# Five warm-up matmuls, not eight; GpSimd takes half of the first split; four maxima units and the projections of batch 1 change places

## What is computed

```python
def _L0_cond_ref(Efou, y, weight):
    ys = y * scale
    d = jax.lax.rsqrt(jnp.einsum('bi,io->bo', ys * ys, weight * weight) + EPS)
    return jnp.einsum('bsi,io->bso', Efou * ys[:, None, :], weight) * d[:, None, :]

def _L0_attn_ref(x, w_qkv, w_out):
    qkv = x @ w_qkv.T
    q, k, v = jnp.split(qkv, 3, axis=-1)
    ...
    q = _apply_rope(q.astype(jnp.float32), cos, sin).astype(x.dtype)
    k = _apply_rope(k.astype(jnp.float32), cos, sin).astype(x.dtype)
    scores = jnp.einsum('bhsd,bhtd->bhst', q, k) / scale
    scores = jnp.where(causal[None, None], scores, -jnp.inf)
    attn = jax.nn.softmax(scores.astype(jnp.float32), axis=-1).astype(x.dtype)
    out = jnp.einsum('bhst,bhtd->bhsd', attn, v)
    ...
    return out @ w_out.T
...
    x = x + _L0_attn_ref(_L0_cond_ref(x, cond_1024, L0_cond_weight), L0_attn_w_qkv, L0_attn_w_out)
    x = x + _L0_ffn_ref(_L0_cond2_ref(x, cond_1024, ...), ...)
```

## Time and profile before

| | |
|---|---|
| runs | 181.8, 184.19 and 183.96 us, median 183.96 us |
| span of the profiled execution | 180.1 us, from the first instruction to the last |
| what lies around the span | 1.7 us (to the fastest run) to 4.1 us (to the slowest); 3.9 us to the median |
| busy in the span | PE 169.0 us (94%), DVE 139.3 (77%), ACT 134.4 (75%), POOL 93.4 (52%) |
| chain that ended last | PE 70%, DVE 14%, ACT 8% of the span |

### The profile page before, as it was taken

The page is one execution under the profiler, slowest core; times in us unless marked ns, Lnnn a source line. Parts: engine busy times, 40 slices in busy tenths (PEclk is TensorE's granted clock), DMA queues, the critical chain, the costliest instruction groups (busy, mean ns, idle before and its releaser), DMA issues.

```text
span 180.1 us, 3258 instructions
## 1 busy us (share of the span) xinstructions
PE 169.0 (94%) x934; PEld 116.8 (65%) x934; DVE 139.3 (77%) x444; ACT 134.4 (75%) x224; POOL 93.4 (52%) x116
## 2 busy tenths in 40 slices
PE   6998989999999999988999999996999989999992
PEld 2765555765666666654648767874677867788881
DVE  5598899789898989981586998699889648637551
ACT  3569366687787788889735696953969999999970
POOL 4508188975453969696541632021769931676000
PEclk9999999999999999999999999999999999999999
DMA  4824673776666756421110799970760000001001
GB/s 132 305 46 103 179 208 118 231 257 233 177 203 187 198 181 184 157 78 49 58 55 9 217 294 361 338 229 11 234 233 0 0 4 0 0 2 58 0 4 58
DMA packets 15349, 24.28 MB, mean 135 GB/s; under 512 B 2844, under 2 KB 4828, under 8 KB 15308
## 3 DMA queue, kind: packets, MB, share of 16 engines
q1 hardware_dynamic: 14532, 23.29, 42.0%
q10 hardware_dynamic: 800, 0.79, 1.7%
HBM read 18.71 MB, written 5.27 MB: 133 GB/s over the span
## 4 chain that ended last, share of the span: by engine, by line
PE 70%; DVE 14%; ACT 8%; issue 5%; POOL 1%; ACTq 0%; DVEq 0%; POOLq 0%
PE psum L1405 11%; PE psum L1538 10%; PE psum L1466 9%; PE psum L1539 9%; PE psum L1540 9%; PE psum L1441 7%; DVE psum L772 4%; PE psum L1341 2%; PE psum L1355 2%; PE psum L1287 2%; ACT t_probs L1105 2%; PE psum L1445 2%; DVE t_raw L924 1%; PE psum L1400 1%; ACT t_q_pad L1155 1%
## 5 line engine op out<-in xcount | busy, mean ns | idle before, releaser
L772 DVE CUSTOM_DVE_ANT_0 psum<-psum,t_causal 128x128 f32<-128x128 f32 (+3 forms) x128 | 58.8, 525 | 6.0 <-PE psum L1405 3.3
L1105 ACT ACTIVATE t_probs<-psum 128x1024 f32<-128x1024 f32 (+2 forms) x48 | 40.8, 883 | 8.4 <-PE psum L1441 5.5
L1405 PE MATMUL psum<-t_stacked,t_q_pad 96*128 96x256 f32 (+2 forms) x104 | 32.1, 378 | 2.4 <-DVE t_row_max L772 1.2
L1405 PEld LDWEIGHTS psum<-t_stacked,t_q_pad 96*128 96x128 f32 x104 | 17.7, 188 | 16.3 <-DVE t_row_max L772 11.2
L672 POOL TENSOR_SCALAR_AFFINE_SELECT t_probs<-t_probs 128x512 f32<-128x512 f32 x32 | 20.5, 653 | 9.0 <-ACT t_probs L1105 8.3
L944 DVE SCALAR_TENSOR_TENSOR t_q_pad<-psum,t_zw_all,t_q_pad 128x512 fp32r<-128x512 f32 x24 | 17.8, 748 | 9.4 <-ACT t_q_pad L1153 9.3
L1139 ACT ACTIVATE psum<-psum 128x512 f32<-128x512 f32 x40 | 23.4, 586 | 1.2 <-PE psum L1540 0.6
L703 POOL TENSOR_TENSOR t_q_pad<-t_raw,t_q_pad 128x512 fp32r<-128x512 f32 x8 | 10.8, 1358 | 21.0 <-ACT t_q_pad L1155 21.0
L1466 PE MATMUL psum<-t_probs,t_v_all 128*32 128x512 f32 (+3 forms) x256 | 20.6, 439 | 0.0
L772 DVE DVE_READ_ACCUMULATOR2_ANT t_row_max<- 128x1 f32 x128 | 18.2, 142 | 0.0
L1153 ACT ACTIVATE t_q_pad<-psum,t_zw_all 128x512 fp32r<-128x512 f32 x24 | 16.5, 689 | 1.2 <-PE psum L1540 0.5
(11 more groups left out here) (232 smaller groups left out, 366.2 us busy)
## 6 DMA issues: line engine op xcount, KB each, us to landing
t_stacked<-scratch SPq DMA_DIRECT2D x16, 256.0 KB, 5.7
t_probs<-in_L_ffn_Wa SPq DMA_DIRECT2D x2, 1024.0 KB, 13.1
scratch<-t_o_sb SPq DMA_DIRECT2D x7, 256.0 KB, 2.0
t_raw<-in_experts SPq DMA_DIRECT2D x7, 256.0 KB, 3.1
t_stacked<-scratch SPq DMA_DIRECT2D x9, 192.0 KB, 2.7
t_q_pad<-scratch SPq DMA_DIRECT2D x28, 48.0 KB
scratch<-t_dn_hi SPq DMA_DIRECT2D x2, 512.0 KB, 3.2
t_q_two<-scratch SPq DMA_DIRECT2D x5, 192.0 KB, 2.6
```

What stands on the lines that cost most here:

```text
L772: last = V.tensor_tensor_reduce(scores, scores, causal[:, S - width:S], 1.0, 3 * BIG, ALU.add, ALU.max, row_max[s][:, qb, j:j + 1])
L1105: A.activation(o, scores, ACT.Exp, scale=float(1.0 / np.sqrt(np.float32(HD)))).then_inc(exp_done, 1)
L1405: last = T.matmul(bank[:, o:o + width], q_pad[s][0:TOP, j, qb * P:(qb + 1) * P], stacked[0:TOP, n, 0:width], start=True, stop=True)
```

## The change

`WARM` goes from 8 to 5. On DVE each of q and k of half 0 is rotated and added before the next, and DVE no longer adds or splits half 1: two additions and two subtractions of 128x256 go to POOL, ahead of its memsets. On PE units 0 to 3 of the maxima stand ahead of `stack_half(0, 1)` and `stack_half(1, 1)`; `project(0)` moves from ahead of unit 0 to behind unit 5, `project_v(0)` from behind unit 6 to behind unit 7, and `project(1)` from behind unit 11 to behind unit 9. On ACT `modulated(1)` moves from ahead of the first `place_q0` to behind the four of half 0, and the spill of the keys moves from ahead of `copy_projection(1)` to behind it.

```diff
-RING_ORDER = [("max", 0, _u) for _u in range(7)] + [("v", 0)] + ...
+RING_ORDER = [("max", 0, _u) for _u in range(8)] + [("v", 0)] + ...
-WARM = 8
+WARM = 5
@@ POOL
-            pool.wait_ge(lo_ready, 4)
+            second = slice(S2, S)
+            for i in range(2):
+                pool.wait_ge(rope_ready, 3 + i)
+                G.tensor_tensor(roped[:, i, second], rope_t[i][1][:, 0, :], rope_t[i][1][:, 1, :],
+                                ALU.add).then_inc(roped_ready, 1)
+            for i in range(2):
+                pool.wait_ge(hi_ready, 3 + i)
+                G.tensor_tensor(qk_lo[:, i, second], roped[:, i, second], f32_of(qk_hi[:, i, second]),
+                                ALU.subtract).then_inc(lo_ready, 1)
             G.memset(v_all[:], 1.0).then_inc(v_ones, 1)
@@ DVE
-            for h in range(2):
-                if h:
-                    dve.wait_ge(ld_rotb, 16)
-                rotate(0, h)
-                rotate(1, h)
-                add_turned(0, h)
-                add_turned(1, h)
-                take_low(0, h)
-                take_low(1, h)
+            for i in range(2):
+                rotate(i, 0)
+                add_turned(i)
+            take_low(0)
+            take_low(1)
+            dve.wait_ge(ld_rotb, 16)
+            rotate(0, 1)
+            rotate(1, 1)
@@ ACT
-            modulated(1, xc[:, 1, :], psum[:, 2, :])
             place_q0(0, 0)
             copy_k0(0)
+            place_q0(1, 0)
+            place_q0(2, 0)
             take_hi_half(0, 1)
-            place_q0(1, 0)
+            place_q0(3, 0)
             take_hi_half(1, 1)
-            place_q0(2, 0)
-            place_q0(3, 0)
+            modulated(1, xc[:, 1, :], psum[:, 2, :])
+            place_q0(0, 1)
             copy_k0(1)
-            for j in range(HG):
+            for j in range(1, HG):
                 place_q0(j, 1)
...
             copy_v(0)
+            copy_projection(1)
             spill(act, 2, NG, 1, spilled)
-            copy_projection(1)
@@ PE, stack_half
-                    pe.wait_ge(rope_ready, i + 1)
+                    pe.wait_ge(rope_ready, 3 + i)
@@ PE
-            project(0)
-            scores_for_max(0, 0)
+            for u in range(HG):
+                scores_for_max(0, u)
             stack_half(0, 1)
             stack_half(1, 1)
-            for u in range(1, len(MX_UNITS[0])):
+            for u in range(HG, len(MX_UNITS[0])):
                 scores_for_max(0, u)
-                if u == 6:
+                if u == 5:
+                    project(0)
+                if u == 7:
                     project_v(0)
-            project(1)
+                if u == 9:
+                    project(1)
```

More of the change, by code:

```diff
@@ L72, in max_units @@
     return MX_LIST[first + (end - first) * i // SLICES:first + (end - first) * (i + 1) // SLICES]
-RING_ORDER = [("max", 0, _u) for _u in range(7)] + [("v", 0)] + [("max", 0, _u) for _u in range(7, len(MX_UNITS[0]))]
+RING_ORDER = [("max", 0, _u) for _u in range(8)] + [("v", 0)] + [("max", 0, _u) for _u in range(8, len(MX_UNITS[0]))]
 RING_ORDER += [("max", 1, _u) for _u in range(2)] + [("lay", 0)] + [("max", 1, _u) for _u in range(2, FIRST)]
@@ L752, in rotate, with add_turned, take_low @@
                                 ALU.mult).then_inc(rope_ready, 1)
-            def add_turned(i, h):
-                dve.wait_ge(rope_ready, 2 * h + i + 1)
-                V.tensor_tensor(roped[:, i, half(h)], rope_t[i][h][:, 0, :], rope_t[i][h][:, 1, :],
+            def add_turned(i):
+                dve.wait_ge(rope_ready, i + 1)
+                V.tensor_tensor(roped[:, i, half(0)], rope_t[i][0][:, 0, :], rope_t[i][0][:, 1, :],
                                 ALU.add).then_inc(roped_ready, 1)
-            def take_low(i, h):
-                dve.wait_ge(hi_ready, 2 * h + i + 1)
-                V.tensor_tensor(qk_lo[:, i, half(h)], roped[:, i, half(h)], f32_of(qk_hi[:, i, half(h)]),
+            def take_low(i):
+                dve.wait_ge(hi_ready, i + 1)
+                V.tensor_tensor(qk_lo[:, i, half(0)], roped[:, i, half(0)], f32_of(qk_hi[:, i, half(0)]),
                                 ALU.subtract).then_inc(lo_ready, 1)
```

## The result

The changed kernel takes **189.03 us** (median of 4 runs, 188.54 to 190.66). The kernel before, on the same chip, takes 182.93 us (4 runs, 181.8 to 184.19). The ratio is 1.035, with a 95% interval of 1.028 to 1.043: slower, where the forecast was 184.8 us and no measurable change. The time lies outside the range.

A forecast was written before the change was run, and what follows sets the result against it. The bound was PE's first unit of group 2 (29.59 us), awaiting DVE's maxima and the padded queries' DMA. Late padded queries decided: span 180.1 + 0.8 = 180.9, plus 3.9 around it, 184.8 us; range 182.0 to 186.8.

The forecast's parts named there:

- part 4: Batch 1's projections among group 0's units: no longer covered by PE's idle time, so the group's maxima are 0.45 us later.
- the clock rises late: Rival at L1341: PE still at 1.2 GHz for half its matmuls gives 186.4 us, for all 188.2; chance 0.13.
- part 1: Three fewer warm-up matmuls: DVE's scaling begins at 5.7 instead of 6.37, a gain of 0.67 us.
- parts 2 to 4: New order up to group 0's maxima: by DVE's path the first unit of group 2 goes out at 29.56 + 0.35.
- part 5: Keys' stores on ACT go 2.2 us later, padded queries of group 2 0.95 us later; +0.8 us taken.
- Part 2: DVE and ACT up to unit 0: its reduction begins at 12.4 instead of 14.65, 2.25 us earlier.
- Part 3: Half 1 through POOL: 0.69 us per 128x256 piece, subtractions end at 14.3 as before, nothing saved there.
- both spills at once: Rival: queries' and keys' stores go at the same moment, landing takes 1 to 1.5 us more: 186.3 us; chance 0.12.

The follow-up runs named there:

- e13: The whole change, with matmuls on zeros filling PE's waits: 183.63 and 183.59 us where the clock stayed up, 186.65 and 187.18 us where it didn't.
- e3: The kernel before with five warm-up matmuls instead of eight, nothing else: 182.91 us (180.82 to 185.27, 5 runs).
- e14: The changed kernel with eight warm-ups and PE's waits filled with matmuls on zeros, keys' stores still behind the copy: 185.55 us, ratio 1.017.
- e7: The changed kernel with the first projection, ACT's modulation copy and the keys' stores back in their old places: 185.8 us, ratio 1.016.
- e6: The changed kernel with the first projection back ahead of unit 0 and ACT's modulation copy back ahead of the slots: 186.56 us, ratio 1.022.
- e5: The changed kernel with the keys' stores on ACT back ahead of the second projection's copy: 189.28 us.
- e2: The changed kernel with eight warm-up matmuls again: 189.14 us (4 runs).
- e4: The kernel before with only the first projection of batch 1 moved behind unit 5: 184.63 us, ratio 1.016.
- e12: The kernel before with the first projection moved behind unit 5 and PE's waits filled with matmuls on zeros: 183.32 us, ratio 1.001.
- e1: The changed kernel with 15 matmuls on zeros (128x512) on PE around units 0 to 3 and the stackings: 187.51 us, ratio 1.030.

## Why the prediction was wrong

**The step that failed** is the sentence that opens part 4: PE "was idle for most of 11.3 to 15.2, which is where the first projection used to be", and from there each pass of the projections was priced at 0.43 us. That idle time was counted as lost cover and nothing more, and the clock in it was put at nothing without a reason. But with the projection in it PE was busy 2.73 of 3 us in 12 to 15 us, without it 1.97 (so it isn't idle for most of the time even then), and the low clock followed: four passes took 3.41 us in the chain instead of 1.71. The rival "the clock rises late" put the clock's danger at L1341 alone and only at its first rise; that it can fall again, in the pause that the change itself makes, stands nowhere. The prediction cited the Trainium skill (TensorE: Matmul & The Clock Gate, Part 1) for that first rise. The same part says that the gate goes by how busy PE has recently been, which is as much a rule for the second; this case's rows agree in that (0.51 behind 1.97 of 3 us), with the exceptions named at the end.

The forecast's base hides a second error. It added 3.9 us for what lies around the span, the difference of the profiled span to the median of three runs. In the later runs of the kernel before, 1.7 to 1.8 us lie around the span, in those of 184.2 us too (span 182.5, clock 0.98). So some 2.2 of the 3.9 us were most likely a fall of the clock in two of the three runs, and the sum for a kernel that keeps its clock is 182.6 us, not 184.8.

The sum with the clock held, from medians and the two runs of `e13` that kept the clock:

| part | said | measured |
|---|---|---|
| five warm-ups (part 1) | -0.67 | -0.8 (181.38 - 182.18), and -0.9 in two runs of `e3` |
| order, parts 2 to 4, without it | +1.0 (0.35 + 0.67) | +0.9 (183.12 - 182.18) |
| late stores on top (part 5) | +0.45 (0.8 - 0.35) | +1.3 (183.6 - 183.12 + 0.8), without a fall; +1.5 in the fastest run of `e14` |
| whole change, clock up | +0.8 | +1.8 (183.6 - 181.8), of which up to 0.4 are the filling matmuls |
| clock, and what its fall brings with it | 0 | +5.4 (189.0 - 183.6) |

- **Part 1.** Right in size: DVE's scaling at 5.59 (5.7 said), L1349 at 6.13 (6.2 said). Its danger was named rightly and weighed too lightly: the sixteen matmuls took 4.74 us in the changed kernel, 5.63 in `e7` and 5.89 in `e6`, about 1.0 to 2.2 us lost, as the late-clock rival had it.
- **Part 2.** Unit 0 at 13.50 instead of 12.4; 1.0 of the 1.1 us is that late rise.
- **Part 3.** Right in size: POOL took 0.72 us each (0.69 said), and the last subtraction ended at 15.24, 0.9 later than forecast, with the late rise before it.
- **Part 4.** Right with the clock held, to 0.2 us at units 0, 4 and 6. In the changed kernel the same places are wrong: unit 6 waited 2.95 us instead of 1.1, since L1363 took 3.4 us in the chain instead of 1.7.
- **Part 5.** The mechanism was right: the stores go behind `project(1)`, and `pad_q(2)` waits for them. The term was too small. It took the landing from another moment (3.7 us); at the new place, with the clock up, it is 5.2, and `pad_q(2)` goes at 27.90 in `e13` instead of 26.4, which was the rival "both spills at once", and PE's wait can bring the clock down. In the changed kernel itself the late stores cost nothing further (three of four runs of `e5`).

That holding the clock gives back the 5.4 us is shown by the filled kernels, each beside its own without filling (189.03 to 183.6, `e2` 189.14 to `e14` 185.55, `e4` 184.63 to `e12` 183.32); how it divides over the three low stretches (the first rise, 15 to 22, 29 to 39 us) is not: `e4` alone gives 1.8 for one of them (2.9 - 1.1). The whole change could not be kept at the high clock in every run, so its +1.8 rests on two runs.

## What to carry to other kernels

When work is moved out of a pause of PE, price the pause as well: look at the windows of PE's busy time and granted clock, and ask what the moved work kept up. A few matmuls of zeros in the waits (0.4 us here) show whether a slowdown is the order's or the clock's, and may be worth keeping. Take the landing time of a moved store from a moment at which its new neighbours are in flight.

## What was unexpected of the hardware

- Short waits are enough. In the changed kernel no wait of PE in 12 to 15 us is longer than 0.7 us, and the clock still fell behind them.
- The same busy time doesn't always end alike. `e13` stood at 1.90 of 3 us in 30 to 33 us in the run profiled and kept its clock there, while `e14` fell at 1.62 and the changed kernel behind 1.97 and 2.11; `e1` kept it behind 1.79 in 24 to 27 us and lost it behind 1.96 in 30 to 33. What decides in between was not tried.
- The kernel before stands at that edge too: its two levels, 181.8 and 184.2 us, went away with the filling matmuls (11 runs of 181.66 to 182.58). What looked like noise of 2.4 us in the runs before the change was most likely this; those runs have no clock on record.
- With five warm-ups the first rise comes at another moment in each profile: the sixteen matmuls of batch 0's projection took 3.82 us (`e13`), 4.74 (the changed kernel) and 5.63 (`e7`) in programs whose PE does the same up to there. In all eight kernels profiled with eight warm-ups they took 3.72.
- The mean granted clock doesn't tell the time. Two of the changed kernel's four runs had 0.981 and 0.982 instead of 0.955 and still took 188.5 and 188.6 us. By an estimate from these figures (mean clock times span), the 186.65 us run of `e13` (0.991) was at the low level for 3.3 us, which costs at most 1.7 us of work, yet it took 3.0 more than the two that kept the clock. A late first rise, which the mean leaves out, and the waits that follow from lost time could fill the gap; those runs were not profiled.
